# Clearing a 37-stage kernel's semaphores in batches of up to 112, with one all-engine barrier between stages in place of two

## The reference

```python
x = L0_attn_x
x = x + 0.5 * _L0_ffn_ref(_layernorm(x), lut, gate_idx, up_idx, down_idx)   # weights from a table of 16 values
x = x + _L0_attn_ref(_layernorm(x), w_qkv, w_out, ln_scale, ln_bias)        # fourth-power attention
x = x + 0.5 * _L0_ffn_ref(...)
x = x + 0.5 * _L1_ffn_ref(...)      # 8 experts, top 2, and a shared expert
x = x + _L1_attn_ref(...)           # latent attention, 16 heads
x = x + 0.5 * _L1_ffn_ref(...)
x = x + 0.5 * _L2_ffn_ref(...)      # 64 experts, top 6, and a shared expert
x = x + _L2_attn_ref(...)           # gated delta rule, 16 heads, a scan over the tokens
x = x + 0.5 * _L2_ffn_ref(...)
x = x + 0.5 * _L3_ffn_ref(...)      # 4-bit weights with low-rank parts
x = x + _L3_attn_ref(...)           # attention over compressed blocks
x = x + 0.5 * _L3_ffn_ref(...)
return x
```

## Time and profile before

| | |
|---|---|
| median of 3 runs | 2215.23 us |
| lowest and highest | 2211.37 and 2226.61 us |
| the profiled execution | 2214.98 us |
| its span | 2213.2 us |
| PE busy | 1847.7 us, 83% |
| DVE busy | 1218.2 us, 55% |
| ACT busy | 879.8 us, 40% |
| POOL busy | 473.0 us, 21% |
| mean granted clock of PE | 0.907 |
| instructions | 52159 |

### The profile page before, as it was taken

How to read it: one execution, slowest core, us unless ns; L and a number is a source line. 1 busy time by engine, 2 the same in 40 slices (tenths; PEclk the granted TensorE clock), 3 DMA queues, 4 the chain that set the end, 5 groups by cost and what they waited for, 6 DMA issues and landing times. The chain is left out here.

```text
span 2213.2 us, 52159 instructions
## 1 busy us (share of the span) xinstructions
PE 1847.7 (83%) x21053; PEld 1275.8 (58%) x21053; DVE 1218.2 (55%) x3265; ACT 879.8 (40%) x2049; POOL 473.0 (21%) x542
## 2 busy tenths in 40 slices
PE   4886789895999896666999999999999797679669
PEld 1345644563777563554766666666676674446446
DVE  6867532344664336645566666676666226642741
ACT  4523311222552222224666677667666203220120
POOL 0022300330000332642212221222121003720200
PEclk7897989996999997887999999999999798789779
DMA  7000000514200516751000010001000317830000
GB/s 266 18 1 1 1 1 16 176 39 156 111 1 19 177 37 215 246 217 51 21 33 22 22 42 22 22 22 42 22 22 22 84 27 218 262 148 18 1 3 19
DMA packets 55331, 157.37 MB, mean 71 GB/s; under 512 B 12899, under 2 KB 29881, under 8 KB 50822
## 3 DMA queue, kind: packets, MB, share of 16 engines
q1 hardware_dynamic: 45206, 128.84, 17.5%
q0 software_dynamic: 9888, 25.20, 3.4%
HBM read 115.36 MB, written 40.48 MB: 70 GB/s over the span
## 5 line engine op out<-in xcount | busy, mean ns | idle before, releaser
L2362 PE MATMUL l_heads_ps_p<-xnT,l2a_w 128*128 128x512 f32 x512 | 266.3, 636 | 20.5 <-ACT l_heads_shaped L2681 8.1
L2768 DVE SCALAR_TENSOR_TENSOR l_heads_taps<-l_heads_padded,l2a_conv,l_heads_taps 128x1024 f32<-128x1024 f32 x144 | 187.9, 1323 | 9.7 <-ACT l_heads_taps L2595 8.9
L2362 PEld LDWEIGHTS l_heads_ps_p<-xnT,l2a_w 128*128 128x128 f32 x512 | 87.4, 194 | 84.3 <-issue 57.9
L198 PE MATMUL norm_turn<-zeros,ident 128*128 128x512 f32 x120 | 65.1, 698 | 52.1 <-PEq L60 52.1
L2941 POOL TENSOR_TENSOR l_heads_e<-l2a_table,l_heads_row 128x512 f32<-128x512 f32 x32 | 33.3, 1042 | 327.1 <-DVE l_heads_first L2779 325.3
L189 ACT ACT_TABLE_LOAD x10 | 12.8, 1283 | 204.1 <-PEq L60 204.1
L2594 ACT COPY l_heads_padded<-l_heads_ps_p 128x512 f32<-128x512 f32 x96 | 57.1, 595 | 53.6 <-PE l_heads_ps_p L2362 53.6
L2595 ACT ACTIVATE l_heads_taps<-l_heads_ps_p,l2a_conv 128x512 f32<-128x512 f32 x96 | 76.7, 799 | 0.0
L198 PEld LDWEIGHTS norm_turn<-zeros,ident 128*128 128x128 f32 x120 | 25.9, 224 | 85.5 <-issue 85.5
L1984 ACT ACTIVATE l_heads_e<-l_heads_logit,l_heads_shift 128x128 f32<-128x128 f32 (+1 forms) x128 | 56.6, 443 | 44.7 <-DVE l_heads_shift L2016 44.6
L2944 POOL TENSOR_SCALAR_AFFINE_SELECT l_heads_e<-l_heads_e 128x512 f32<-128x512 f32 x64 | 67.0, 1047 | 9.8 <-POOL l_heads_e L2941 0.6
(11 more groups left out here) (717 smaller groups left out, 4833.8 us busy)
## 6 DMA issues: line engine op xcount, KB each, us to landing
l_results<-zeros SPq DMA_DIRECT2D x24, 512.0 KB, 5.7
l_ffn_a_w_in<-in_l_in_w SPq DMA_DIRECT2D x8, 1536.0 KB
l_ffn_b_w_in<-in_l_in_w SPq DMA_DIRECT2D x8, 1536.0 KB, 10.5
l2a_w<-in_l_w_heads SPq DMA_DIRECT2D x16, 512.0 KB, 3.9
l_heads_row<-l_rows SPq DMA_DIRECT2D x16, 512.0 KB, 4.6
l_ffn_a_w_out<-in_l_out_w SPq DMA_DIRECT2D x8, 768.0 KB
l_ffn_a_w_in<-l_results SPq DMA_DIRECT2D x8, 768.0 KB, 6.5
l_ffn_b_w_out<-in_l_out_w SPq DMA_DIRECT2D x8, 768.0 KB, 8.3
```

Source lines behind the costliest of these rows:

```text
L198: pe.matmul(turn[:, i % KC, (i // KC) % HALVES, :], core.ident[:], core.zeros[:, 0:HALF], start=True, stop=True)
L2362: mm = pe.matmul(ps_p[half][:], w[b][:, which, c, :], core.xnT[:, c, half * HALF:(half + 1) * HALF], start=(c == 0), stop=(c == KC - 1))
L2768: dve.scalar_tensor_tensor(out=taps[which][:], in0=padded[which][:, :, j:j + SEQ], scalar=conv[p % 2][:, which, j:j + 1], in1=taps[which][ ...
```

## The change

A stage no longer clears its semaphores when it ends: it leaves them, uncleared and still allocated, in the list `Stage.over`. When a later stage asks for a semaphore and the ones left over and its own so far are 112 or more, POOL clears all that were left over, and an all-engine barrier follows. This happens while the stage allocates, ahead of its block. After a stage's last block barrier nothing else is emitted.

```diff
+COUNTED = 112
+
 class Stage:
+    over = []
 ...
     def sem(self, name):
+        if Stage.over and len(Stage.over) + len(self.sems) >= COUNTED:
+            self.nc.clear_and_free_semaphores(Stage.over)
+            self.nc.all_engine_barrier()
+            Stage.over = []
         s = self.nc.alloc_semaphore(f"{self.name}_{name}_{self.seen}")
 ...
     def __exit__(self, *failed):
         if failed[0] is None:
             self.blocks.close()
-            self.nc.clear_and_free_semaphores(self.sems)
-            self.nc.all_engine_barrier()
+            Stage.over = Stage.over + self.sems
             self.ctx.close()
 ...
+    Stage.over = []
     build(nc, t, out)
```

## The result

The changed kernel takes 2202.47 us, the median of 7 runs (2199.16 to 2205.67), against 2215.23 (2211.37 to 2226.61, 7 runs). The ratio is 0.9928, with a 95% interval of 0.9905 to 0.9951: a gain of 0.5 to 1.0%. The ratio stands for 16 us, while the two medians lie 12.8 apart. The forecast was 2205.5. The profiled execution is 2200.06 us with a span of 2198.3.

What follows compares the result with a forecast made beforehand. The prediction took the 37 stages to be in series, so the time between them is added whole. Removing 18.4 us and adding 8.7 nets 9.7: 2215.2 - 9.7 = 2205.5 us, range 2202 to 2209 (8 in 10: 2198 to 2213).

Steps and rivals of the forecast that it cites:

- The stages are in series and each stretch counts in full: Stage ends: the first-to-second-barrier stretch, 0.50 us a stage, lies wholly on the path, since every engine waits in it.
- 18.4 us removed: At 37 stage ends: drains, range clears and second barriers go, 18.4 us over the program, 0.83% of the time.
- 8.7 us added, of three terms: Five longer stretches with 29 range clears over 465 semaphores: 2.0 + 3.8 + 2.9 = 8.7 us.
- term 3: In the five clearings: 465 semaphores, 2.5 us at 5.3 ns each, bound 3.7, taken as 2.9 us.
- term 2: In the five clearings: 24 further ranges at 0.16 us each for drain, clear's fixed part and two gaps, 3.8 us.
- 360 ns as the longest clear: POOL's range clears in the new profile: longest near 39 + 5.3 x 60 = 360 ns.
- The bounds, 6.3 to 11.1: Net gain of 9.7 us: 11.1 if later drains cost nothing, 6.3 if each is as long as the longest, 202 ns.
- The clears themselves are not saved; the barrier is what costs: Stage ends: 480 semaphores cleared before, 465 after, 2.5 us stays; the barrier is the larger part of a 0.4 us stretch.
- Rival C: The five clearings cost more: drains of 0.2 us and a late engine in each stretch, gain 5 to 6, 2210; chance 0.08.
- Rival A: Stage starts: the second barrier covered instruction fetch; stalls at up to 32 ends, 12.8 against 9.7, gives 2218; chance 0.07.
- Rival D: Stage starts: nothing saved, because engines or transfers would have waited anyway; 2215; chance 0.04.
- rival B: PE's clock decides: a half-clock stretch costs up to 8 us, 2213 or 2198, no sign; chance 0.13, half each way.

Runs made afterwards that it cites:

- the ring: The changed kernel with stage semaphores numbered round and round in 138 to 253, five clearings in 9 ranges instead of 29; 2200.12 us in its only run.

## Why the prediction was right, and by what it was short

*The stages are in series and each stretch counts in full.* Right. The stretches fell by 9.7 us, and none of it was taken back by a transfer or a late engine.

*18.4 us removed.* Right: 18.43 and 18.28 in two traces of the kernel before.

*8.7 us added, of three terms.* Right in the sum, 8.73. The terms come out of the trace as they were put. The 29 clears last 3.53 us, of which 1.13 is their fixed part and 2.4 the semaphores; the 29 drains last 2.27 us, some 0.5 more than 29 of 60 ns would, because the ones ahead of large clears are longer (182 ns ahead of the 502 ns clear). With the 2.4 this makes the 2.9 of term 3. A further range is 0.06 + 0.04 + 0.03 + 0.03 = 0.16 us where its clear is small, as in term 2, and the ring's 0.13 comes from longer drains and one late gap. What the prediction had wrong is the shape: it named 360 ns as the longest clear, and one range held 87 semaphores and took 502. The bounds, 6.3 to 11.1, were wider than needed.

*The clears themselves are not saved; the barrier is what costs.* Right, and shown: with all 37 barriers put back and the batches kept, the gain is gone.

*Rival C, a costlier clearing.* Wrong: the median drain in the clearings is 71 ns, not 200, and no engine comes late in the five stretches.

*Rival A, code fetch behind the missing cover.* Wrong everywhere: PE's first matmul comes as soon behind L66's release as it did behind L60's, 0.12 us at 32 of 36 starts and at the other four as before to within 0.4 us. The two late drains of the kernel before did not come back in the five stretches that are left, whose PE and DVE drains are all 13 and 19 ns long. The Trainium skill (Runtime: NRT & Kernel Launch, Instruction fetch mechanics) has its stall only for a branch that leaves the fetched window; no jump between stages shows one on PE here that the kernel before did not have too.

*Rival D,* that the time would have been waited anyway: wrong, by the sum.

*The clock (rival B) "has no sign".* **This is where the prediction fell short:** the term for PE's clock, put at nothing, is 3 to 9 us. I gave the gain in the stretches as the whole gain and the clock a symmetric scatter, with only a slight leaning. Three comparisons of the changed kernel gave 0.9928, 0.9929 and 0.9932, 15 to 16 us each; taken as independent, with half-widths near 0.0025, they average 0.9930 with a half-width of 0.0015, a gain of 12 to 19 us. That leaves out 9.7. The two comparisons of the kernel with no stretches at all gave 21 and 26 us against 18.4 (the first interval holds 18.4, the second doesn't). Adding 37.8 us of idle stretches cost 51.6. In all three the time moved by more than the stretches, in the mean of each by a factor of 1.3 to 1.6. What the runs show of the cause: PE's idle time at stage ends lowers its clock in the next stage, and filling it gives some 30 us back. At doses of 38 us and more this is shown. That the same mechanism makes the 3 to 9 us surplus of the change itself is in part inferred, from its direction and size. Single traces scatter too much to read it there; over all runs low clock was 17 us less in one comparison (9 each way) and 3 less in the other (15 each way), so the first shows it and the second leaves it open. The median of the first comparison, 12.8 us, is the low end of what the change is worth.

The time itself, 2202.47, lay just inside the range of 2202 to 2209, and within 1% of the time before, which had 0.93. The first of these was in part luck: with a gain of 15 to 16 us from 2215.2 it would have been below 2201, outside that range though inside 2198 to 2213.

**A version that is faster still.** The clears beside the next stage, with no second barrier: ratios 0.9903 and 0.9883, against 0.9928 to 0.9932 for the change. It needs the semaphores of two neighbouring stages at once, not 112, and each number is reused only behind the next block barrier, which POOL reaches after its clear.

## What to carry to other kernels

Where stages are in series, count the fixed cost of their ends from the releases in the trace, and separate what needs all engines (a barrier) from what one idle engine can do beside the next stage (a clear): moving the clear off the path was worth more than doing it less often. Time in which every engine waits may be lost more than once: in this kernel TensorE's clock was lower with more of it, the stages behind it paid again, and the idle time saved was less than the gain. Whether that is so elsewhere is to be read from the granted clock of several runs, not of one trace. When a batch is made of things that used to be handled one by one, ask whether they still lie together, since each break in the run of numbers has its own price.

## What the runs showed of the hardware

- A range clear on POOL takes about 39 ns and some 5.3 for each semaphore in its range: 44 ns for 1, 67 for 6, 308 for 51, 502 for 87, 608 for 106. Batching does not make it cheaper: the clears last 3.87 us in total before and 3.53 after.
- The drain that stands ahead of a range clear is mostly longer when the clear is large: 64 ns ahead of 6 semaphores, 182 ahead of 87, 274 at most with the ring. The size is not all of it: drains of 184, 192 and 217 ns stand ahead of clears of 44 and 45 ns where the clears run beside the next stage. Why is open.
- A bare all-engine barrier behind another is 0.33 us (95 of 111 and 32 of 37), and 0.36 to 0.77 otherwise, so 0.34 to 0.37 in the mean: 37.8 us for 111 of them, 13.7 for 37.
- Six matmuls of 128x128 f32 at each stage's end took 65.6 us of stretches and cost 38 to 39 in the end, because the rest, with the clock higher (0.917 to 0.919 in five runs against 0.902 to 0.907 in nine), was some 30 shorter.
